# Sums and squares of x1 taken from the addition and from ScalarE, x's statistics begun a unit earlier, and the spectral stage's output stored in eight pieces

## What is computed

```python
x = x + _L0_conv_ref(_gn(x), ...)   # min-max scaling, box sums of sizes 2, 4, 8, 16, logs, slope over the sizes
x = x + _L1_conv_ref(_gn(x), ...)   # cosine/Fourier modes, mixed per mode, transformed back, plus x @ W.T + b, relu
x = x + _L2_conv_ref(_gn(x), ...)   # 7 x 7 blur
x = x + _L3_conv_ref(_gn(x), ...)   # as L1, with 64 x 64 modes

def _gn(v, G=16, eps=1e-5):
    g = v.reshape(B_, H_, W_, G, C_ // G)
    m = jnp.mean(g, axis=(1, 2, 4), keepdims=True)
    s = jnp.var(g, axis=(1, 2, 4), keepdims=True)
    return ((g - m) / jnp.sqrt(s + eps)).reshape(v.shape)
```

## Time and profile before

| | |
|---|---|
| median of three runs | 8006.95 us |
| profiled execution, time and span | 7989.88 us, 7988.3 us |
| fractal stage in the profile | 0 to about 3400 us |
| spectral stage in the profile | about 3540 to 4760 us |
| busy share of the span | PE 84%, DVE 70%, ACT 46%, POOL 4% |

### The profile page before, as it was taken

How to read it: one execution, slowest core, us unless ns; L and a number is a source line. 1 busy time by engine, 2 the same in 40 slices (tenths; PEclk the granted TensorE clock), 3 DMA queues, 4 the chain that set the end, 5 groups by cost and what they waited for, 6 DMA issues and landing times. The chain is left out here.

```text
span 7988.3 us, 106283 instructions
## 1 busy us (share of the span) xinstructions
PE 6738.2 (84%) x35680; PEld 4253.5 (53%) x35680; DVE 5621.8 (70%) x10505; ACT 3650.5 (46%) x4902; POOL 343.4 (4%) x274
## 2 busy tenths in 40 slices
PE   5888888888888888949999969999999999636998
PEld 2544455444444445537767745565666666523443
DVE  8989999898999999746666655555554555366665
ACT  4667777666666666812222213434343434201121
POOL 0000000000000000010000000000000000000101
PEclk9889988888989898969999989999999999667999
DMA  1111111111111111175555567767676766399999
GB/s 79 71 71 71 71 70 71 59 55 49 58 66 71 71 71 71 61 221 201 180 186 200 169 201 178 179 168 179 163 180 162 183 161 174 110 327 281 316 334 305
DMA packets 781384, 1176.65 MB, mean 147 GB/s; under 512 B 200306, under 2 KB 682082, under 8 KB 764354
## 3 DMA queue, kind: packets, MB, share of 16 engines
q1 hardware_dynamic: 628162, 916.80, 37.6%
q10 hardware_dynamic: 133120, 140.54, 6.7%
q0 software_dynamic: 19712, 114.31, 3.6%
HBM read 706.59 MB, written 464.91 MB: 147 GB/s over the span
## 5 line engine op out<-in xcount | busy, mean ns | idle before, releaser
L432 PE MATMUL a_PS<-a_H,a_band 128*128 128x448 f32 x5120 | 2227.6, 593 | 398.4 <-DVE a_H L537 320.4
L432 PEld LDWEIGHTS a_PS<-a_H,a_band 128*128 128x128 f32 x5120 | 1045.2, 210 | 1422.2 <-issue 1214.8
L1230 PE MATMUL d_PS<-d_N,d_Bd 128*128 128x504 f32 x3072 | 1375.5, 600 | 81.0 <-ACT d_R L1337 58.3
L361 ACT ACTIVATE a_L<-a_PS,a_eps 128x896 f32<-128x896 f32 x1024 | 1025.1, 1001 | 593.7 <-PE a_PS L432 592.9
L1230 PEld LDWEIGHTS d_PS<-d_N,d_Bd 128*128 128x128 f32 x3072 | 577.4, 194 | 735.7 <-issue 732.5
L1413 DVE TENSOR_TENSOR d_X<-d_R,d_X 128x504 f32<-128x504 f32 x512 | 347.8, 679 | 878.9 <-ACT d_R L1337 877.2
L370 ACT ACTIVATE a_X<-a_L,a_alp 128x224 f32<-128x224 f32 x1024 | 816.2, 797 | 7.6 <-DVE a_L L546 7.6
L1088 DVE SCALAR_TENSOR_TENSOR c_XO<-c_PS,c_XC 128x128 f32<-128x128 f32 x1792 | 471.0, 407 | 414.7 <-PE c_PS L960 406.4
L1337 ACT ACTIVATE d_R<-d_PS,d_b 128x504 f32<-128x504 f32 x512 | 347.3, 681 | 782.1 <-PE d_PS L1230 671.9
L544 DVE TENSOR_TENSOR a_L<-a_L 128x1792 f32<-128x1792 f32 x256 | 517.2, 2020 | 247.8 <-ACT a_L L361 246.1
L1541 DVE TENSOR_TENSOR e_OUT<-e_PS,e_X 112x224 f32<-112x224 f32 x1024 | 430.1, 538 | 261.7 <-PE e_PS L1495 160.9
(11 more groups left out here) (185 smaller groups left out, 7412.7 us busy)
## 6 DMA issues: line engine op xcount, KB each, us to landing
d_X<-tmp_x SPq DMA_DIRECT2D x512, 252.0 KB, 5.0
a_X<-in_x SPq DMA_DIRECT2D x32, 3584.0 KB, 19.1
c_XC<-tmp_x SPq DMA_DIRECT2D x224, 512.0 KB, 4.4
tmp_x<-d_X SPq DMA_DIRECT2D x512, 204.8 KB
tmp_x<-a_X SPq DMA_DIRECT2D x32, 3136.0 KB, 18.0
tmp_x<-c_XO SPq DMA_DIRECT2D x32, 3136.0 KB, 18.7
d_XR<-tmp_x ACTq DMA_DIRECT2D x256, 392.0 KB, 5.6
e_X<-tmp_x SPq DMA_DIRECT2D x128, 784.0 KB, 15.6
```

Of the source, the lines that this page charges most:

```text
L361: act.activation(out, PS[:, b0:b0 + 2, 0:2 * W], ACT.Ln, bias=eps[:, 0:1]).then_inc(sem["ln_done"], 1)
L432: last = pe.matmul(PS[:, 2 * (j % 2) + k, 0:2 * W], band[:, pos, :], Hb[:, u % 2, level, y1:y1 + HALF, :].rearrange("p y c -> p (y c)"), s ...
L1230: last = pe.matmul(PS[:, c % 2, 0:NW], Bd[:, c * 3 + s, :], N2[:, c % 4, :, s:s + NY], start=(s == 0), stop=(s == 2))
```

## The change

In the fractal stage:

- `add` becomes two instructions of 448 elements a row that also sum their results into `total` (one number per row and pair of channels).
- `stats_of_x1` goes. In its place ScalarE's new `squares_of_x1` takes two `Square` activations per unit with `total` as bias and a sum into `spread`, at the end of the unit in front of `put_back`. Their elementwise results go to a part of `L` that nothing reads any more.
- `hand_over` (VectorE, end of unit 2) turns both sums into the table that `bn_stats` used to fill; the copy L111 goes.
- The chain of x1's statistics comes one unit later (means in unit 3 instead of 2, and so on).
- `stats_of_x` runs in units 3 to 9 instead of 4 to 10, and the chain of x's statistics one unit earlier, with `cf` at the end of unit 13.

In the spectral stage SP stores each sample's x2 in eight pieces of 784 KB, one after each of the loads in units 0 to 7 of the next sample; the last sample's pieces follow its last unit.

```diff
             def logs(s, u, j):
                 if j == 0:
                     after(act, sem["z_ready"], U(s, u) - 1)
+                    after(act, sem["x_back"], U(s, u) - 2)
...
+            def squares_of_x1(s, u):
+                cg, t = divmod(u, T)
+                after(act, sem["x1_ready"], U(s, u) + 1)
+                square = L[:, (u + 1) % 2, 1].rearrange("p y c -> p (y c)")
+                for j in range(2):
+                    g = 2 * cg + j
+                    last = act.activation(square[:, COUNT * j:COUNT * j + COUNT], X1[:, u % 4, :, 2 * j:2 * j + 2], ACT.Square,
+                                          scale=-float(COUNT), bias=total[:, s.par, t, g:g + 1],
+                                          accum_out=spread[:, s.par, t, g:g + 1])
+                if u == UN - 1:
+                    last.then_inc(sem["spread_done"], 1)
...
                     if cur and u >= 2:
+                        squares_of_x1(cur, u - 2)
                         put_back(cur, u - 2)
                     elif prev and u < 2:
+                        squares_of_x1(prev, UN - 2 + u)
                         put_back(prev, UN - 2 + u)
...
             def add(s, u):
-                dve.tensor_tensor(X1[:, u % 4], X1[:, u % 4], X[:, s.par, t, :, cg * CG:cg * CG + CG], ALU.add)\
-                   .then_inc(sem["x1_ready"], 1)
+                for j in range(2):
+                    g = 2 * cg + j
+                    mine = X1[:, u % 4, :, 2 * j:2 * j + 2]
+                    last = dve.scalar_tensor_tensor(out=mine, in0=mine, scalar=1.0,
+                                                    in1=X[:, s.par, t, :, 2 * g:2 * g + 2], op0=ALU.mult, op1=ALU.add,
+                                                    accum_out=total[:, s.par, t, g:g + 1])
+                last.then_inc(sem["x1_ready"], 1)
...
-                        if u > 1 and cur and level <= 2:
-                            stats_of_x1(cur, u - 2, level - 1)
-                        if u < 2 and prev and level <= 2:
-                            stats_of_x1(prev, UN - 2 + u, level - 1)
...
-                    if nxt and 4 <= u <= 10:
-                        for k in range(2 * (u - 4) + (u == 10), 2 * (u - 4) + 2 + (u >= 9) + (u == 10)):
+                    if nxt and 3 <= u <= 9:
+                        for k in range(2 * (u - 3) + (u == 9), 2 * (u - 3) + 2 + (u >= 8) + (u == 9)):
                             stats_of_x(nxt, k)
...
+            def store(e, par, piece):
+                t, ph = divmod(piece, NP)
+                r0 = PADR + t * (H // 2)
+                sp.dma_start(d["x2"][e, r0:r0 + H // 2, ph], XO[ONCE[t], par, t, ph]).then_inc(sem["stored"], 16)
...
-                for t in range(T):
-                    r0 = PADR + t * (H // 2)
-                    sp.dma_start(d["x2"][e, r0:r0 + H // 2], XO[ONCE[t], par, t]).then_inc(sem["stored"], 16)
+                    if prev is not None and n < PIECES:
+                        store(prev, 1 - par, n)
```

More of the change, by code:

```diff
@@ L232, in pass_fractal @@
         sx = GroupStats(z.sb, "sx", T, W)
-        s1 = GroupStats(z.sb, "s1", T, W, ahead=True)
+        s1 = GroupStats(z.sb, "s1", T, W)
+        total = z.sb("total", [P, 2, T, G])
+        spread = z.sb("spread", [P, 2, T, G])
+        COUNT = 2 * W
         PS = z.ps("PS", [P, 8, 512])
@@ L481, in body @@
                           .then_inc(sem["sx_out"], 1)
-                    if nxt and u == 14:
+                    if nxt and u == 13:
                         after(pe, sem["sx_in"], nxt.e * 4 + 4)
@@ L551, in add, with hand_over @@
                 after(dve, sem["z_ready"], U(s, u) + 1)
-                dve.tensor_tensor(X1[:, u % 4], X1[:, u % 4], X[:, s.par, t, :, cg * CG:cg * CG + CG], ALU.add)\
-                   .then_inc(sem["x1_ready"], 1)
-            def stats_of_x1(s, u, j):
-                cg, t = divmod(u, T)
-                if j == 0:
-                    after(dve, sem["x1_ready"], U(s, u) + 1)
-                g = 2 * cg + j
-                last = dve.bn_stats(s1.rows[:, t, g, :], X1[:, u % 4, :, 2 * j:2 * j + 2])
-                if u == UN - 1 and j == 1:
-                    s1.hand_over(dve, steps, last, sem["s1_in"])
+                for j in range(2):
[5 more added lines that the diff above has]
+                last.then_inc(sem["x1_ready"], 1)
+            def hand_over(s):
+                after(dve, sem["spread_done"], s.e + 1)
+                bn = s1.bn[:].rearrange("p s g v -> p (s g) v")
+                for of, first, scale in ((total, 1, 1.0 / COUNT), (spread, 2, 0.5 / COUNT / COUNT)):
+                    last = dve.tensor_scalar(bn[:, :, first:6:3],
+                                             of[:, s.par].rearrange("p s g -> p (s g)").unsqueeze(2)
+                                             .to_broadcast([P, T * G, 2]), scale, None, ALU.mult)
+                last.then_inc(sem["s1_in"], 1)
             def stats_of_x(s, k):
@@ L605, in body @@
                 for u in range(UN):
-                    if prev and u == 3:
+                    if prev and u == 4:
                         after(dve, sem["s1_out"], prev.e * 3 + 1)
                         s1.dve_deviations(dve, steps, ST1, sem["s1_in"])
-                    if prev and u == 5:
+                    if prev and u == 6:
                         after(dve, sem["root_out"], root_count(prev, False))
@@ L616, in body @@
                         last.then_inc(sem["s1_in"], 1)
-                    if prev and u == 6:
+                    if prev and u == 7:
                         after(dve, sem["s1_out"], prev.e * 3 + 3)
@@ L620, in body @@
                         steps.done(dve.tensor_copy(keep.bcol1[:, bass.ds(prev.e, 1)], ST1[:, 65:66]))
-                    if nxt and u == 12:
+                    if nxt and u == 11:
                         after(dve, sem["sx_out"], nxt.e * 4 + 1)
                         sx.dve_deviations(dve, steps, STX, sem["sx_in"])
-                    if nxt and u == 14:
+                    if nxt and u == 13:
                         after(dve, sem["sx_out"], nxt.e * 4 + 3)
@@ L820, in pass_spectral @@
     UNITS = PAIRS * T
+    PIECES = T * NP
+    STORED = 16 * PIECES
     RING = 7
@@ L874, in load @@
                   .then_inc(xin[n % RING], 16)
+            def store(e, par, piece):
+                t, ph = divmod(piece, NP)
+                r0 = PADR + t * (H // 2)
+                sp.dma_start(d["x2"][e, r0:r0 + H // 2, ph], XO[ONCE[t], par, t, ph]).then_inc(sem["stored"], 16)
             def body(e, par, prev, nxt):
                 if e is None:
+                    sp.wait_ge(sem["f_done"], prev * UNITS + UNITS)
+                    for piece in range(PIECES):
+                        store(prev, 1 - par, piece)
                     return
@@ L891, in _ @@
             turns(sp, body)
-            sp.wait_ge(sem["stored"], B * 32)
+            sp.wait_ge(sem["stored"], B * STORED)
         @block.gpsimd
@@ L1080, in body @@
                     if n == 0:
-                        after(dve, sem["stored"], e * 32 - 32)
+                        after(dve, sem["stored"], e * STORED - STORED)
                     if n == 3 and nxt is not None:
```

28 lines of the change are left out of this document (15 added, 13 removed).

## The result

The changed kernel takes 7971.32 us (median of 11 runs, 7961.14 to 7982.17), the kernel before 7996.15 us beside it (11 runs, 7984.83 to 8008.19). The ratio is 0.9971, with a 95% interval of 0.9964 to 0.9979: faster by 0.3%, a little over the 0.2% that can be told from no change. The forecast was 8025 us, slower by 0.2%. The measured time lies in its range, on the other side of no change. The profiled execution of the changed kernel took 7971.97 us, with a span of 7970.4 us against 7988.3.

The account below looks back on a forecast made before the run. VectorE was taken to bound fractal units with x's statistics, TensorE and ScalarE plain units, load waits to cost TensorE spectral time. Fractal +113 and spectral -95 made +18 us: 8025 us on the median, range 7930 to 8115.

Parts of the forecast that it names:

- TensorE's wait for the extremes: Fractal stage, unit 12: the 1.87 us wait stays and grows, with a lower clock behind it; unit 12 takes 13.6 us.
- Spectral stores: Spectral stage: pieces remove all 77.1 us of TensorE's load waits and slower restarts, -95 us, bounds 0 and -110.
- The wait in unit 3: Fractal stage: VectorE waits some 10 us for x's load in each of 14 samples, 140 us in all.
- VectorE's stretch: Fractal units with x's statistics: dropping bn_stats outweighs dearer additions and x1's chain moving in, 2.9 us gained a sample.
- the price of the additions: VectorE, fractal stage: a pair of summing additions costs 1.28 us, between 1.08 and 2.02, against 1.01 for one before.
- The tail: Fractal units 10 to 15: 65.8 us instead of 57.0, 8.8 more a sample.
- First and last sample: Fractal stage: the last sample's plain units add 14 us; the first, with its x at once, gains 3.
- the fractal term: Whole fractal stage: +113 us, from +7.3 a sample 14 times, +14 and -3; bounds +50 to +170.
- the first (squares hidden in plain units): Fractal stage: plain units stay at 9.3 us because TensorE closes them, 7933 us in all; chance 0.24.
- The second: Spectral stage: pieces hold up loads, so half of the gain is left, 8072 us in all; chance 0.11.
- the fourth: Fractal unit 3: loads land sooner, so statistics don't wait; 10 us gained a sample, 7885 us in all; chance 0.05.
- The third: VectorE, fractal stage: summing additions run at half pace, 2.02 + 0.2 us instead of 1.28, +85, 8110 us; chance 0.08.

Follow-up runs that it names:

- first kernel: Kernel before with only the spectral stage's eight store pieces: 7888.77 us, ratio 0.9875 to the kernel before.
- eighth kernel: Kernel before with its two whole x2 stores issued in units 0 and 4 of the next sample, not in pieces: 7879.56 us, ratio 0.9851.
- fifth kernel: Changed kernel with tile 0 of x1 stored after its own last put_back, a unit before tile 1: 7833.36 us, ratio 0.9796 to the kernel before.
- third: Kernel before with only x's statistics and their chain one unit earlier, bn_stats of x1 kept: 8078.12 us, ratio 1.011.
- sixth kernel: Changed kernel without the squares of 15 of the 16 units of x1: 7930.01 us, ratio 0.9915 to the kernel before.
- seventh kernel: Kernel before with x's statistics a unit earlier, tile 0 of x1 stored early and spectral pieces, bn_stats of x1 kept: 7823.52 us, ratio 0.9789.
- ninth kernel: Fifth kernel with the previous sample's third group of column products moved from unit 0 to unit 2: 7795.07 us, ratio 0.975 to the kernel before.
- tenth kernel: Seventh kernel with TensorE's step for the extremes moved behind unit 12's column and row products: 7747.89 us, ratio 0.9696 to the kernel before.

## Why the prediction was wrong, and where it was right

Most mechanisms came as written, and one did not: TensorE's wait for the extremes became shorter where I had it grow. The sum was too dear by 36 us (8008 for the profiled execution, 7972 measured, both against 7990 before), and that was enough to turn a small gain into a small loss. Of the 54 us between 8025 and 7971, another 11 are the base, as the median of three runs before stood that much above the median of eleven; the rest is the scatter of the two profiled executions around their medians. Step by step:

1. **Spectral stores: right.** -95 forecast, -98.5 measured; the first kernel shows it alone. The reason was right as well, though the eighth kernel shows that the eight pieces are not needed for it.
2. **The wait in unit 3: right.** Some 10 us in 14 samples, 140 in all, were forecast; it is 135.7 us, 135.0 of them in unit 3 of these 14 samples. The distance from stores to statistics stayed at 33 us, and the start of the statistics moved by +1.3 us instead of +1.4 (from unit 1's combination 35.7 us before, 37.0 now). The fifth kernel, in which only the place of a store is moved, ends the wait.
3. **VectorE's stretch: too dear by 0.9 us a sample.** -2.9 forecast; from the first statistics to the combination behind the last it went from 105.3 to 101.5, -3.8. The term that failed is the price of the additions. I took 1.28 us for a pair, with 0.10 for each sum; the timeline above has starts 0.54 and 0.55 us apart, 1.09 a pair, within 0.01 of the lower bound that I had kept. The sum's own instruction (83 ns) starts together with the next one and takes nothing from the queue. Six additions at 0.19 are 1.1 us. The three box sums without `bn_stats` between them gained 0.81 us a unit where I had 0.85 (from the first sum's start to the combination's in a unit of sample 5: 4.19 before, 3.38 now), which takes back 0.3.
4. **The tail: too dear by 1.6 us a sample.** 65.8 forecast for units 10 to 15, 64.2 measured. Units 10, 11 and 13 to 15 came close to the forecast (8.7, 10.7 and 32.3 together, against 9.0, 11.1 and 32.1). For the last three this is partly luck: I had added 1.4 us to 9.3, and it is 1.2 on 9.5. Unit 12 took 12.5 instead of 13.6. I had written that TensorE's wait for the extremes stays and grows, and had put a lower clock behind it. It shrank, from 31.0 us in the run to 22.9, as the squares make TensorE late for it. It grew only where there are no squares, to 49.8, 42.5 and 49.6 us (third, sixth and seventh kernel), and there unit 12 takes 14.6, 14.3 and 16.4 us in the mean. The sixth kernel is the changed one less the squares, so it is they that shorten the wait. So the squares' cost in the tail and the longer wait exclude each other, and I had put one on top of the other.
5. **First and last sample.** The last one took 162.7 us instead of 148.6, the +14 forecast; the first -5.7 instead of -3.
6. **Not foreseen: unit 2**, 9.5 to 12.4 us. Squares make ScalarE late there too. TensorE has neither column nor row products in that unit and stands idle for 3.05 us in sample 5, and the clock of the unit is 0.86. It cost nothing here, as the wait in unit 3 swallowed it: the loads set the end of both. Without that wait unit 2 takes 13.7 us, and 10.8 with its idle time filled (fifth and ninth kernel).

Terms 3 and 4 are 2.5 us a sample, 35 us in 14 samples, and the first sample is 3 more: nearly all of the 40 us by which the fractal term, +113 forecast and +73.4 measured, was too dear. So this term is the failed step, in two places: a pair of summing additions priced at 1.28 us that costs 1.09, and a unit 12 put at 13.6 us, with a growing wait and a lower clock, that takes 12.5 with a shorter wait at clock 1.00. The spectral term was too cautious by 3.5 us, and against both stand 7 us in the mixing stage and elsewhere that I had put at nothing. The measured term lies within the bounds that I had given it (+50 to +170), but the sum stood only 18 us, one unit of what can be told from no change, above zero, while its largest term had bounds 120 us apart; half of the chance on slower was more than such a sum bears.

Of the rivals, the first (squares hidden in plain units) is refuted: three plain units take 32.1 us, and the sixth kernel has them short again. That the kernel came out faster, as this rival had it, is for another reason: terms 3 and 4. The second fell with the first kernel, the fourth with the wait.

The third was half pace for the additions. From start to start they take 0.54 us each, as `bn_stats` over the same 448 elements did. The Trainium skill, "Vector Engine (DVE) Microarchitecture Reference", section "7. Points that are easy to get wrong", has this operation with two SBUF sources that aren't bf16 at half throughput; the trace disagrees, with the accumulator as without it. The Trainium skill, "VectorE: DVE Perf Modes", section "Two Vector instructions with no wait between them", says that an operation which also writes out its accumulator is two instructions; the trace agrees (the rows of L575), and shows in addition that here the second one costs no time of the queue.

## What to carry to other kernels

Before work is moved to an earlier place, look when its data lands: here one unit earlier turned a transfer that came just in time into a wait of 10 us, and moving one store ahead was worth six times the change itself. A wait on TensorE can cost twice, once for its length and, as in most samples of unit 12 without squares, once more for a lower clock behind it. So look for instructions that don't wait and put them ahead of the one that does; a unit in which TensorE idles can become shorter by getting more work, as unit 2 did. When two costs lean on the same slack (here slower units and an early arrival at a wait), price them together, and don't let a sum decide whose bounds are several times its size.

## What the runs showed of the hardware

A sum written by VectorE's addition is an instruction of its own of 83 ns that took no time of the queue: starts of the pair 1183.56 and 1184.10, the sum's read at 1184.10 as well. ScalarE's is not free: its record is 197 ns beside 703 for the square, and it holds the queue for 0.09 us (starts 1339.39 and 1339.48), so that two squares with their sums take 1.39 us. Plain units grew by 1.2 us (9.6 to 10.8 in unit 13, sixth kernel against the changed one).

TensorE's granted clock fell in units in which it had stood and waited. In unit 2 it was 0.75 in the fifth kernel, where ten products took 7.05 us behind a wait of 3.04, and 1.00 in the ninth, where the same ten took 4.03 behind a wait of 1.28. In unit 12 it was 0.72 to 0.88 in the samples shown in which TensorE had come early to a wait, and 1.00 where the wait stood behind its products. In the sixth kernel 16 column products took 3.68 us at clock 0.50 behind a wait of 2.42 us in sample 6, but 2.05 behind a wait of 2.61 in sample 5; in the changed one 2.05 behind a wait of 1.43. The Trainium skill, "TensorE: Matmul & The Clock Gate", section "HAM oscillation — how this bites in real kernels", advises, where matmuls wait for loads, an order of work that doesn't let TensorE idle between short runs of them; the ninth and tenth kernel, where the waits are for other engines, agree, with 0.5% and 0.9% of the whole time (0.9796 to 0.975, 0.9789 to 0.9696).

Between the loads the store's size made no difference that can be told: eight pieces of 784 KB gave 0.9875 [0.9856, 0.9894], two stores of 3136 KB set apart 0.9851 [0.9838, 0.9864]. Small pieces in the old place were not tried.
